# Layer norm ahead of attention: the statistics of the next image spread over units 7 to 22, the root replaced by a power of -0.5 on GpSimd

## The chip, the cores and the metric

The kernel runs on one core of a Trainium2 chip. The metric is the device time of one execution in microseconds (us). "Image" below is one of the eight 32x32 images with 384 channels (1,024 pixels each), numbered 0 to 7.

## The reference, cut to what matters

Three stages follow each other, each over all eight images. A convolution of group-normalised features comes first, and a feed-forward block comes last; neither is touched. The change is in the middle stage, attention with 12 heads of 32 channels:

```python
def _ln_t(v, eps=1e-05):
    m = jnp.mean(v, axis=-1, keepdims=True)
    s = jnp.var(v, axis=-1, keepdims=True)
    return (v - m) / jnp.sqrt(s + eps)

t = _to_tokens(x)                       # (8, 1024, 384)
t = t + _L1_attn_ref(_ln_t(t), Wq, Wk, Wv, Wo, bo)
```

The layer norm is over the 384 channels of each pixel. In the attention, q, k and v are projections of the normalised tokens, the softmax is over the 1,024 keys, and the result goes through Wo.

## The kernel before, in words

`attention_stage` keeps channels on the 128 partitions (three chunks, KC) and pixels on the free axis, in two halves of BANK = 512 pixels. After a prologue, which loads weights, normalises image 0 and projects it, each image goes through 24 **units** (`unit`, lines 966, 1143, 1277, 1375). A unit treats four heads, 256 queries and 512 keys in two halves e = 0, 1. Each engine runs its own hand-written list, and semaphores tie the lists together:

- TensorE, in each half: four score products (`scores`, L903) into two PSUM banks in turn, so that product n waits for exponential n-2; then `weigh` (L936, L944), which multiplies an earlier half's exponentials with v and with ones; then a `wave` (L919) of later scores into the four-bank tile `mx`.
- ScalarE: eight exponentials (L1232) of 128x512. VectorE: per half one `reduce_max` of `mx` (L1066); the next wave waits for it, as `mx` has one copy. GpSimd: four additions of exponentials (`add_pair`, L1356), which `weigh` waits for one unit later.

Other work lies between these. Units 6 to 23 project the next image (`project`, 18 items of nine 512-column products or of the same in 128-column pieces), through the single bank `pj`. Items come in threes of pairs q, k, v; the v items stand in units 10, 11, 16, 17, 22 and 23. ScalarE moves each item out (`stage_high`), VectorE takes the low part of q and k (`stage_low`, L1059). In units 6 to 21 an item is cut into four pieces that stand around the third score product of both halves; in 22 and 23 all of it stands in the first half. Units 0 to 5 put the previous image through Wo (`out_project`, L887), all in the second half; `move_out` takes it from `pj`, and GpSimd adds it (L1330). On odd units `move_pv` (L1240) copies `pv` and VectorE inverts the sums (`invert_sum`); on even units follow `attended` (VectorE), `attended_high` (ScalarE) and `attended_low` (GpSimd, L1320).

The layer norm of the image after the next takes these steps, for each half h of 512 pixels:

- `load_x` (SyncE, in unit 6) waits for the low parts of the image before. `fold_x` (GpSimd, units 18 and 20, L1334, L1337) adds the three chunks; `mean` (TensorE, L834, units 22 and 23) multiplies with 1/384 into `pj`; `centre` (VectorE, L1022) subtracts.
- In units 0 and 1 of the next image ScalarE squares a whole half in one instruction of 128x1536 (`square`, L1189) into the memory of `z[1]`, and GpSimd adds the chunks ahead of the unit's `add_pair` (`fold_squares`). `var` (L840, units 1 and 2) puts the mean square into `pj`, and `root` (L1194) takes the square root on ScalarE, before the fifth exponential of the unit.
- `invert_std` (VectorE, units 2 and 4) turns the root by 32x32 blocks, takes the reciprocal of one column per block (L1032) and turns it back over all columns; `normalise` (L1041) multiplies, units 3 to 5. `z_high` (ScalarE, L1201, units 4 and 5) rounds a whole half to float16, and `z_low` (VectorE, L1047, units 4 to 6) takes what is left. The projections of unit 6 on read both.

`schedule` (L689) writes units 6 to 23 of image b and 0 to 5 of image b+1 as the body of a loop, run six times; image 0's units 0 to 5 stand before it, and the rest of images 6 and 7 after it. The loop's jump lies between units 5 and 6. Image 7's units have no layer norm, and its units 6 to 23 no projection. The last image whose layer norm is made, image 7, is normalised in image 6. The prologue's end makes both means of image 1 (L961) before unit 0.

```python
for e in range(2):                                   # unit on TensorE, before
    scores(b, u, e, 0)
    if norm and u in (1, 2) and e == 0:
        var(b + 1, u - 1)
    if load and u >= IU - 2 and e == 1:
        mean(b + 2, u - IU + 2)
    scores(b, u, e, 1)
```

## Time and profile before

| | us |
|---|---|
| median of 3 runs (range) | 3006.07 (3001.13 to 3012.16) |
| the profiled execution, its own time | 3010.64 |
| its span, first to last instruction | 3008.7 |
| TensorE busy, matmuls | 2672.3 (89%) |
| VectorE busy | 1847.6 (61%) |
| ScalarE busy | 1586.1 (53%) |
| GpSimd busy | 1370.8 (46%) |
| mean granted TensorE clock | 0.949 |

The profiled execution took 1.9 us more than its span. Attention's first exponential starts at 475.64 us and its last at 2167.4 us. A unit is measured from its first exponential to that of the next unit; the boundaries 475.64, 685.80, 904.20, 1122.55, 1341.05, 1559.48, 1776.40 and 1986.60 are those of images 0 to 7. The clock column of a window is the share of full speed that was granted to TensorE, where 1.00 is 2.4 GHz and 0.5 is 1.2 GHz.

### The profile page before, as it was taken

To read this page: it belongs to the slowest core of one execution; us is meant where nothing else is said; L and a number is where in the kernel's file an instruction comes from. 1 tells how busy PE (TensorE), PEld (TensorE's weight loads), DVE (VectorE), ACT (ScalarE), POOL (GpSimd) and SP (SyncE) were. 2 spreads that over 40 slices of the span, in tenths; PEclk is the share of its full clock that TensorE was granted. 3 is DMA by queue.
4 is the path that set the end of the run, shared out by engine and by line. 5 is a ranking of instruction groups with operands and counts; after the bars stand their busy time and mean duration, and the time that the engine had idled before them with its cause. 6 is when DMAs were issued, how large, how long until landed. Compare 5 with 4: busy or idle time off the path is not lost. (4 is left out here: it accounts for less than half of the span.)

```text
span 3008.7 us, 64263 instructions
## 1 busy us (share of the span) xinstructions
PE 2672.3 (89%) x23600; PEld 1302.3 (43%) x23600; DVE 1847.6 (61%) x2360; ACT 1586.1 (53%) x2582; POOL 1370.8 (46%) x1096
## 2 busy tenths in 40 slices
PE   4989756998997997998988988998859999999999
PEld 3555322453453453543543544543324444444444
DVE  6766246887777787887777778777433333333332
ACT  2323024666666665666666666666534444444443
POOL 2222034676676676676676677677620101111110
PEclk9989877999998998998999999999979999999999
DMA  4233232111211211212112112111020101101010
GB/s 149 87 115 106 79 97 83 51 30 30 93 30 48 74 35 60 61 36 83 39 36 83 41 30 71 42 30 43 1 105 22 43 25 38 42 21 42 21 42 21
DMA packets 68634, 164.41 MB, mean 55 GB/s; under 512 B 13569, under 2 KB 17470, under 8 KB 67326
## 3 DMA queue, kind: packets, MB, share of 16 engines
q1 hardware_dynamic: 68350, 160.60, 16.8%
q8 instruction: 181, 2.97, 0.4%
q14 instruction: 103, 0.84, 0.1%
HBM read 59.13 MB, written 37.75 MB: 32 GB/s over the span
## 5 line engine op out<-in xcount | busy, mean ns | idle before, releaser
L1356 POOL TENSOR_TENSOR b_pair<-b_ex 128x512 f32<-128x512 f32 x768 | 975.3, 1295 | 517.9 <-ACT b_ex L1232 516.5
L1232 ACT ACTIVATE b_ex<-b_st 128x512 f32<-128x512 f32 x1536 | 866.4, 596 | 485.2 <-PE b_st L903 464.2
L1066 DVE TENSOR_REDUCE b_mxp<-b_mx 128x4 f32<-128x2048 f32 x384 | 876.9, 2284 | 322.4 <-PE b_mx L919 309.6
L903 PE MATMUL b_st<-b_qst,b_kst 97*128 97x256 f16 (+1 forms) x3072 | 548.0, 282 | 117.5 <-ACT b_ex L1232 83.1
L903 PEld LDWEIGHTS b_st<-b_qst,b_kst 97*128 97x128 f16 (+1 forms) x3072 | 235.1, 99 | 452.1 <-ACT b_ex L1232 255.5
L1601 DVE TENSOR_TENSOR c_gs<-c_g,c_gs 128x512 f16<-128x512 f32 x192 | 132.7, 691 | 482.0 <-ACT c_gs L1674 482.0
L936 PE MATMUL b_pv<-b_ex,b_v 128*32 128x256 f32 x6144 | 422.8, 394 | 0.0
L1522 PE MATMUL c_hid<-c_z,c_wi 128*128 128x512 f16 x1728 | 405.3, 380 | 11.3 <-DVE c_z L1594 11.3
L1537 PE MATMUL c_acc<-c_gs,c_wo 128*128 128x512 f16 x1728 | 404.0, 379 | 0.4 <-DVE c_gs L1601 0.4
L1670 ACT ACTIVATE c_g<-c_hid,c_bias 128x512 f32<-128x512 f32 x192 | 131.4, 684 | 363.5 <-PE c_hid L1522 363.3
L1522 PEld LDWEIGHTS c_hid<-c_z,c_wi 128*128 128x128 f16 x1728 | 169.3, 98 | 227.5 <-issue 18.8
L1537 PEld LDWEIGHTS c_acc<-c_gs,c_wo 128*128 128x128 f16 x1728 | 169.0, 98 | 204.5 <-ACT c_gs L1674 0.9
L944 PE MATMUL b_pv<-b_pair,b_ones 128*32 128x256 f32 x3072 | 241.6, 387 | 0.8 <-POOL b_pair L1356 0.8
L1707 POOL TENSOR_TENSOR c_xs<-c_x 128x512 f32<-128x512 f32 x16 | 21.3, 1334 | 478.6 <-DMA c_x<-after_attention 476.3
L936 PEld LDWEIGHTS b_pv<-b_ex,b_v 128*32 128x32 f32 x6144 | 163.1, 111 | 153.6 <-issue 81.5
L919 PE MATMUL b_mx<-b_kst,b_qst 32*128 32x512 f16 x1536 | 155.5, 395 | 35.9 <-DVE b_mxp L1066 32.4
L887 PE MATMUL b_pj<-b_ao,b_wo 128*128 128x512 f16 x432 | 115.0, 397 | 19.1 <-ACT b_xs L1194 14.7
L944 PEld LDWEIGHTS b_pv<-b_pair,b_ones 128*32 128x32 f32 x3072 | 101.4, 112 | 70.8 <-issue 6.1
L863 PE MATMUL b_pj<-b_z,b_wq 128*128 128x512 f16 x405 | 122.2, 397 | 10.5 <-DVE b_z L1047 7.7
L919 PEld LDWEIGHTS b_mx<-b_kst,b_qst 32*128 32x128 f16 x1536 | 38.8, 91 | 199.6 <-issue 147.1
L1674 ACT ACTIVATE c_gs<-c_g 128x512 f16<-128x512 f32 x192 | 120.9, 630 | 6.2
L308 PE MATMUL a_conv<-a_fs,a_wm 128*128 128x512 f16 x432 | 116.6, 421 | 0.0
(162 smaller groups left out, 2754.1 us busy)
## 6 DMA issues: line engine op xcount, KB each, us to landing
a_x<-in_x SPq DMA_DIRECT2D x8, 1536.0 KB, 6.9
a_ob<-a_x SPq DMA_DIRECT2D x8, 1536.0 KB, 7.2
after_conv<-a_ob SPq DMA_DIRECT2D x24, 512.0 KB, 2.6
b_xl<-after_conv SPq DMA_DIRECT2D x8, 1536.0 KB, 6.9
b_qst<-b_staged0q SPq DMA_DIRECT2D x192, 64.0 KB, 2.0
b_kst<-b_staged0k SPq DMA_DIRECT2D x192, 64.0 KB, 2.0
b_v<-b_vstaged SPq DMA_DIRECT2D x24, 512.0 KB, 3.0
b_xr<-after_conv SPq DMA_DIRECT2D x8, 1536.0 KB, 6.6
```

The lines of the kernel that those rows point to most:

```text
L863: last = nc.tensor.matmul(bank[:, :], ws[kind][a][:, k, g * P:(g + 1) * P], z[b][:, k, part * BANK:(part + 1) * BANK], start=n == 0, stop= ...
L903: last = nc.tensor.matmul(st[n % NST][:, j * QUERIES:(j + 1) * QUERIES], kst[g][0:depth, s, kt * P:(kt + 1) * P], qst[g][0:depth, s, q0:q0 ...
L919: last = nc.tensor.matmul(mx[:, s, :], qst[g][rows, s, q0 + t * P:q0 + (t + 1) * P], kst[g][rows, s, half * BANK:(half + 1) * BANK], start ...
L936: last = nc.tensor.matmul(pv[s * HEAD:(s + 1) * HEAD, 0:QUERIES], v[g][:, kt, s * HEAD:(s + 1) * HEAD], ex[u % 2][e][s][:, j * QUERIES:(j ...
L944: last = nc.tensor.matmul(pv[s * HEAD:(s + 1) * HEAD, QUERIES:BANK], ones[:, :], pair[u % 2][s][:, e * QUERIES:(e + 1) * QUERIES], start=F ...
L1066: nc.vector.reduce_max(mxp[x % 2][:, w // 2, :, w % 2], mx[:, :, :], AX_X).then_inc(mx_taken, 1)
L1232: nc.scalar.activation(ex[u % 2][e][s][:, :], st[n % NST][:, :], ACT.Exp, scale=SCALE).then_inc(exp_ready, 1)
L1356: nc.gpsimd.tensor_tensor(pair[u % 2][s][:, :], ex[u % 2][0][s][:, :], ex[u % 2][1][s][:, :], ALU.add).then_inc(pair_ready, 1)
L1522: last = nc.tensor.matmul(hid[m % NH][:, :], wi[a][:, k, m * P:(m + 1) * P], z[p][b][:, k, :], start=n == 0, stop=n == 8)
L1537: last = nc.tensor.matmul(acc[j][:, :], wo[a][:, m, j * P:(j + 1) * P], gs[m % NS][b][:, :], start=m == 0 and n == 0, stop=m == MC - 1 and ...
L1601: nc.vector.tensor_tensor(gs[m % NS][1][:, :], g[m % NG][:, :], gs[m % NS][0][:, :], ALU.subtract).then_inc(glo_ready, 1)
L1670: nc.scalar.activation(g[m % NG][:, :], hid[m % NH][:, :], ACT.Gelu, bias=bias[:, m:m + 1], scale=1.0 / WSCALE).then_inc(gelu_ready, 1)
```

## The change

Each step of the layer norm is done on one chunk of 512 columns and has a new place. For image b+2, in image b: `fold_x` in units 8 and 9, `mean` and `centre` in 10 and 11, `square` and `fold_square` in 12 to 15, `var` in 16 and 17, the inverse in 16 to 18, `normalise` in 18 to 21. In the next image's units 0 and 1 comes `z_high`, in units 0 to 2 `z_low`. The squares go into `xs` and into `std_turned` instead of `z[1]`. ScalarE's root is gone: VectorE turns the mean square out of PSUM, adds eps to one column per block, GpSimd raises the 128x16 column to -0.5, and VectorE turns it back. On TensorE the statistics stand in the second halves of the v units 10, 11, 16 and 17, whose item is put into the first half; units 22 and 23 are cut like the others; all items are cut 3, 2, 3, 1 instead of 2, 2, 2, 3 products, and the items through Wo are cut over both halves too, but for unit 3, where they stay in the second. In the prologue, image 1's statistics are made between the projections of image 0 through the score banks, and image 1 is normalised at its end; its load is issued ahead of the stacking copies. Waits and counts of semaphores follow.

```diff
+        def stat_bank(m, h):
+
+            return st[h] if isinstance(m, int) and m == 1 else bank_of(m, h)
+
+        def square_scratch(m):
+
+            return ot if in_prologue(m) else std_turned
+
+        V_UNITS = [FIRST + 6 * g + 4 + part for g in range(GROUPS) for part in range(2)]
+        MEAN_AT, VAR_AT = V_UNITS[0:2], V_UNITS[2:4]
...
                 for piece in range(PIECES + 1):
                     stack(0, 1, piece)
                 sp.wait_ge(w_low, 4)
                 load_r(0)
-                load_x(1)
                 sp.wait_ge(rows_set, 4 * GROUPS)
                 load_rows(0, 0)
...
+                    if i in (6, 7):
+                        mean(1, i - 6)
+                    if i in (13, 14):
+                        var(1, i - 13)
                     if i >= NQKV - AHEAD:
                         wave(0, i - NQKV)
...
+                first_half = qkv and u in MEAN_AT + VAR_AT
+                second_half = u == KC
 
                 for e in range(2):
                     scores(b, u, e, 0)
-                    if norm and u in (1, 2) and e == 0:
-                        var(b + 1, u - 1)
-                    if load and u >= IU - 2 and e == 1:
-                        mean(b + 2, u - IU + 2)
                     scores(b, u, e, 1)
-                    if item == 2:
-                        if e == 0:
+                    pieces = (0, 0), (0, 0)
+                    if first_half or second_half:
+                        if e == second_half:
+                            pieces = (0, 5), (5, 9)
+                    else:
+                        pieces = ((0, 3), (3, 5)) if e == 0 else ((5, 8), (8, 9))
+                    if begin and pieces[0][1]:
+                        if pieces[0][0] == 0:
                             if u == FIRST:
                                 pe.wait_ge(exp_ready, FILLS * (IU * b + u) + 1)
                             begin()
-                        part(2 * e, 4)
-                        scores(b, u, e, 2)
-                        part(2 * e + 1, 4)
-                    elif item == e:
-                        begin()
-                        part(0, 2)
-                        scores(b, u, e, 2)
-                        part(1, 2)
-                    else:
-                        scores(b, u, e, 2)
+                        part(*pieces[0])
+                    if load and u in MEAN_AT and e == 1:
+                        mean(b + 2, MEAN_AT.index(u))
+                    if load and u in VAR_AT and e == 1:
+                        var(b + 2, VAR_AT.index(u))
+                    scores(b, u, e, 2)
+                    if begin and pieces[0][1]:
+                        part(*pieces[1])
                     scores(b, u, e, 3)
                     if lagging(b, u, 2 - e):
...
                 if step == 0:
-                    dve.wait_ge(std_ready, 2 * m + h + 1)
-                    nc.vector.transpose(std_turned[:, :], std[h][:, :]).then_inc(inv_ready, 1)
-                if step == 1:
+                    dve.wait_ge(var_ready, 2 * m + h + 1)
+                    if not in_prologue(m):
+                        dve.wait_ge(sq_folded, 4 * m + 4)
+                    nc.vector.transpose(std_turned[:, :], stat_bank(m, h)[:, :]).then_inc(inv_ready, 1)
                     dve.wait_ge(inv_ready, at + 1)
-                    nc.vector.reciprocal(std_col[:, :], one_column(std_turned)).then_inc(inv_ready, 1)
+                    nc.vector.tensor_scalar(std_col[:, :], one_column(std_turned), EPS, None, ALU.add
+                                            ).then_inc(inv_ready, 1)
                 if step == 2:
-                    dve.wait_ge(inv_ready, at + 2)
+                    dve.wait_ge(inv_ready, at + 3)
                     nc.vector.transpose(std[h][:, :], over_columns(std_col)).then_inc(inv_ready, 1)
...
+                    if i in (7, 8):
+                        for k in range(KC):
+                            centre(1, i - 7, k)
+                    if i in (14, 15):
+                        for step in range(INVERSE):
+                            invert_std(1, i - 14, step)
...
                     for k in range(KC):
-                        centre(1, h, k)
+                        normalise(1, h, k)
...
+                    if u % 2 == 0 and n == 1 and lagging(b, u, 4):
+                        attended(b, (u - 4) // 2)
+                    if load and u in MEAN_AT and n >= 5:
+                        centre(b + 2, MEAN_AT.index(u), n - 5)
+                    if load and u == VAR_AT[0] and n >= 5:
+                        invert_std(b + 2, 0, n - 5)
+                    if load and (u, n) in ((VAR_AT[1], 5), (VAR_AT[1], 7), (VAR_AT[1] + 1, 2)):
+                        invert_std(b + 2, 1, (5, 7, 2).index(n))
+                    if load and (u, n) in ((18, 3), (18, 6), (19, 1)):
+                        normalise(b + 2, 0, (3, 6, 1).index(n))
+                    if load and (u, n) in ((19, 2), (20, 6), (21, 1)):
+                        normalise(b + 2, 1, (2, 6, 1).index(n))
                     if u % 2 and n >= 5 and lagging(b, u, 3):
                         invert_sum(b, (u - 3) // 2, n - 5)
-                    if u % 2 == 0 and n == 1 and lagging(b, u, 4):
-                        attended(b, (u - 4) // 2)
-                    if load and u >= IU - 2 and n == 7:
-                        for k in range(KC):
-                            centre(b + 2, u - IU + 2, k)
-                    if not norm:
-                        return
-                    if (u, n) in ((2, 2), (2, 5), (2, 6)):
-                        invert_std(b + 1, 0, (2, 5, 6).index(n))
-                    if (u, n) in ((3, 1), (3, 2), (3, 7)):
-                        normalise(b + 1, 0, (1, 2, 7).index(n))
-                    if (u, n) in ((4, 2), (4, 3), (4, 5)):
-                        invert_std(b + 1, 1, (2, 3, 5).index(n))
-                    if (u, n) in ((4, 6), (5, 2), (5, 3)):
-                        normalise(b + 1, 1, (6, 2, 3).index(n))
-                    if (u, n) in ((4, 7), (5, 1), (5, 7)):
-                        z_low(b + 1, 0, ((4, 7), (5, 1), (5, 7)).index((u, n)))
-                    if (u, n) in ((6, 2), (6, 3), (6, 6)):
-                        z_low(b + 1, 1, (2, 3, 6).index(n))
+                    if norm and (u, n) in ((0, 6), (0, 7), (1, 1)):
+                        z_low(b + 1, 0, (6, 7, 1).index(n))
+                    if norm and (u, n) in ((1, 7), (2, 2), (2, 3)):
+                        z_low(b + 1, 1, (7, 2, 3).index(n))
...
+            def square(m, h, k):
+                act.wait_ge(centred, KC * (2 * m + h) + k + 1)
+                wait(act, sq_folded, 4 * m + 2 * h + max(k - 1, 0))
+                if k == 1 and not in_prologue(m):
+                    act.wait_ge(inv_ready, 2 * NORMED * m)
+                into = xs[h] if k == 0 else square_scratch(m)
+                nc.scalar.activation(into[:, :], xl[:, k, h * BANK:(h + 1) * BANK], ACT.Square
                                      ).then_inc(squared, 1)
 
-            def root(m, h):
-                act.wait_ge(var_ready, 2 * m + h + 1)
-                nc.scalar.activation(std[h][:, :], bank_of(m, h)[:, :], ACT.Sqrt, bias=eps[:, 0:1]
-                                     ).then_inc(std_ready, 1)
...
+            def z_high(m, h, k):
+                act.wait_ge(z_ready, 6 * m + 3 * h + k + 1)
...
+                    if i in (8, 10):
+                        square(1, i // 2 - 4, 0)
+                        square(1, i // 2 - 4, 1)
+                    if i in (9, 11):
+                        square(1, i // 2 - 4, 2)
...
+                def beside(n):
+
+                    if load and 12 <= u < 16:
+                        h, step = u // 2 - 6, u % 2
+                        if n in (1, 5) and (step == 0 or n == 1):
+                            square(b + 2, h, 2 * step + n // 5)
+                    if norm and u < 2 and n in (1, 3, 5):
+                        z_high(b + 1, u, n // 2)
+                    if qkv and u >= FIRST and n == (2 if u in MEAN_AT + VAR_AT else 6):
+                        stage_high(b + 1, u - FIRST)
+                    if u % 2 and n == 3 and lagging(b, u, 3):
+                        move_pv(b, (u - 3) // 2)
+                    if u % 2 == 0 and n == 5 and lagging(b, u, 4):
+                        attended_high(b, (u - 4) // 2)
+                    if u < FIRST and out_proj and n == 7:
+                        move_out(b - 1, u)
+
+                for n in range(FILLS):
+                    exponential(b, u, n // HG, n % HG)
+                    beside(n)
...
+            def fold_square(m, h, k):
+                pool.wait_ge(squared, 3 * (2 * m + h) + k + 1)
+                wait(pool, sq_folded, 4 * m + 2 * h + k - 1)
+                nc.gpsimd.tensor_tensor(xs[h][:, :], xs[h][:, :], square_scratch(m)[:, :], ALU.add
+                                        ).then_inc(sq_folded, 1)
+
+            def invert(m, h):
+                pool.wait_ge(inv_ready, NORMED * (2 * m + h) + 2)
+                nc.gpsimd.tensor_tensor(std_col[:, :], std_col[:, :], power[:, :], ALU.pow).then_inc(inv_ready, 1)
+                pool.wait_ge(inv_ready, NORMED * (2 * m + h) + 3)
...
+                for h in range(HALVES):
+                    for k in (1, 2):
+                        fold_square(1, h, k)
+                for h in range(HALVES):
+                    invert(1, h)
...
-                if norm and u in (0, 1):
-                    fold_squares(b + 1, u)
                 for s in range(HG):
-                    if load and u in (18, 20) and s == 1:
-                        fold_x(b + 2, u // 2 - 9)
+                    if load and u in (8, 9) and s == 1:
+                        fold_x(b + 2, u - 8)
+                    if load and (u, s) in ((VAR_AT[0], 3), (VAR_AT[1], 3)):
+                        invert(b + 2, VAR_AT.index(u))
+                    if load and 12 <= u < 16 and s == 3 - u % 2 * 2:
+                        fold_square(b + 2, u // 2 - 6, 1 + u % 2)
```

## Rows read from the trace of the kernel before

**Rows 1.** Windows, image 3: length, busy us by engine, PEclk; units 0-8, 19, 22.

```profile
core 0: us, PE busy (x) PEld busy (x) DVE busy (x) ACT busy (x) POOL busy (x), PEclk, DMA share, GB/s
1122.55:1133.95 11.40, 8.38 (x82) 3.80 (x81) 10.33 (x11) 6.49 (x12) 8.98 (x9) 0.95 0.20 48
1133.95:1148.69 14.74, 11.40 (x84) 4.48 (x84) 5.37 (x6) 10.14 (x15) 9.55 (x9) 0.81 0.17 42
1148.69:1159.22 10.53, 8.80 (x85) 3.78 (x83) 7.43 (x13) 8.58 (x13) 4.78 (x5) 1.00 0.16 40
1159.22:1167.57 8.35, 7.78 (x83) 3.67 (x81) 8.28 (x8) 5.63 (x11) 7.07 (x8) 1.00 0.16 62
1167.57:1178.86 11.29, 9.35 (x83) 3.99 (x81) 9.88 (x15) 6.62 (x12) 6.63 (x5) 0.85 0.00 1
1178.86:1192.19 13.33, 8.19 (x83) 3.78 (x81) 10.71 (x11) 6.89 (x12) 11.16 (x9) 0.95 0.01 4
1192.19:1204.72 12.53, 11.16 (x83) 4.60 (x82) 8.62 (x14) 5.20 (x11) 3.28 (x3) 0.65 0.68 254
1204.72:1212.57 7.85, 7.78 (x83) 3.67 (x82) 5.88 (x6) 5.64 (x10) 6.03 (x6) 1.00 0.60 205
1212.57:1220.42 7.85, 7.78 (x83) 3.67 (x82) 6.88 (x12) 5.13 (x10) 4.96 (x5) 1.00 0.28 67
...
1298.63:1306.91 8.28, 7.77 (x83) 3.67 (x82) 5.88 (x6) 5.53 (x11) 8.17 (x8) 1.00 0.30 99
...
1323.04:1332.04 9.00, 8.53 (x112) 5.18 (x111) 8.14 (x14) 5.25 (x10) 5.17 (x5) 1.00 0.01 2
```

**Rows 2.** Windows: image 0 units 0-5, image 6 units 0-5 and 6-23, image 7 units 0-5, 6-18.

```profile
475.64:538.70 63.06, 44.38 (x366) 16.50 (x364) 45.62 (x54) 39.54 (x62) 35.20 (x28) 0.74 0.02 8
1776.40:1839.70 63.30, 52.13 (x492) 23.02 (x490) 50.35 (x57) 44.46 (x71) 45.09 (x37) 0.95 0.12 34
1839.70:1986.60 146.90, 140.45 (x1621) 73.56 (x1620) 115.26 (x144) 96.47 (x181) 97.22 (x83) 1.00 0.17 52
1986.60:2036.90 50.30, 46.41 (x486) 21.97 (x486) 34.45 (x43) 32.66 (x60) 38.49 (x34) 1.00 0.16 42
2037.09:2134.23 97.14, 80.29 (x937) 34.17 (x936) 75.34 (x94) 61.39 (x117) 68.55 (x59) 1.00 0.10 34
```

**Rows 3.** Timeline, unit 1 of image 3, PE and ScalarE: the root.

```profile
1139.53 1.28 ACT L1194 ACT_TABLE_LOAD   x1
...
1141.57 1.04 PE L887 MATMUL b_pj<-b_ao,b_wo 128*128 128x512 f16 x4 [2.10 <-ACT b_xs L1194]
```

**Rows 4.** Timeline, TensorE, units 5 to 6 of image 3.

```profile
1191.55 1.03 PE L903 MATMUL b_st<-b_qst,b_kst 97*128 97x256 f16 x4 [3.40 <-issue]
```

**Rows 5.** Instructions by line, VectorE on b_xl: ns min/median/max, first and last start.

```profile
L1041 DVE TENSOR_TENSOR b_xl<-b_xl,b_xs x48: 677/1178/1786, 399.5 to 1834.8; 128x512 f32<-128x512 f32 x48
L1047 DVE TENSOR_TENSOR b_z<-b_xl,b_z x48: 676/706/1777, 406.4 to 1848.3; 128x512 f16<-128x512 f32 x48
L1022 DVE TENSOR_TENSOR b_xl<-b_xl,b_pj x45: 648/677/689, 387.6 to 1776.3; 128x512 f32<-128x512 f32 x45
```

**Rows 6.** Timeline, TensorE's score matmuls, unit 22 of image 3.

```profile
1322.61 0.61 PE L903 MATMUL b_st<-b_qst,b_kst 97*128 97x256 f16 x4
...
1327.37 0.39 PE L903 MATMUL b_st<-b_qst,b_kst 97*128 97x256 f16 x2
```

**Rows 7.** Instructions by line, the reciprocal on VectorE and a GpSimd fold.

```profile
L1032 DVE RECIPROCAL b_std_col<-b_std_turned x16: 230/252/255, 398.5 to 1825.4; 128x16 f32<-128x16 f32 x16
...
L1337 POOL TENSOR_TENSOR b_xs<-b_xs,b_z x16: 1259/1278/2258, 392.5 to 1792.1; 128x512 f32<-128x512 f32 x16
```

**Rows 8.** Timeline, TensorE, end of the prologue and image 0's first scores.

```profile
462.48 0.40 PE L919 MATMUL b_mx<-b_kst,b_qst 32*128 32x512 f16 x4 [0.28 <-DVE b_mxp L1066]
...
474.97 1.06 PE L903 MATMUL b_st<-b_qst,b_kst 97*128 97x256 f16 x4
```

More of the change, by code:

```diff
@@ L769, in prologue @@
                 sp.dma_start(bo[:, :], b_o).then_inc(c_loaded, 16)
+                load_x(1)
                 for piece in range(PIECES + 1):
@@ L823, in _ @@
         def _(pe):
-            free = {id(pj): None, id(pv): None}
+            free = {id(bank): None for bank in (pj, pv, *st)}
             def take(bank, done, count):
@@ L860, in project_part @@
                 if kind < 2:
-                    for n in range(9 * piece // pieces, 9 * (piece + 1) // pieces):
+                    for n in range(n0, n1):
                         (a, b), k = PARTS[n // KC], n % KC
@@ L866, in project_part @@
                 else:
-                    for t in range(4 * piece // pieces, 4 * (piece + 1) // pieces):
+                    for t in range(4 * n0 // 9, 4 * n1 // 9):
                         at = (part * 4 + t) * P
@@ L881, in out_project, with out_part @@
                 pe.wait_ge(alo_ready, done)
-            def out_part(b, i, piece, pieces):
+            def out_part(b, i, n0, n1):
                 h, j = i // KC, i % KC
-                for n in range(9 * piece // pieces, 9 * (piece + 1) // pieces):
+                for n in range(n0, n1):
                     (a, c), k = PARTS[n // KC], n % KC
@@ L889, in out_part @@
                                             start=n == 0, stop=n == 8)
[L890 removed]
+                if n1 == 9:
                     last.then_inc(o_ready, 1)
@@ L972, in unit @@
                 if u < FIRST and out_proj:
                     begin = lambda: out_project(b - 1, u)
-                    part = lambda *piece: out_part(b - 1, u, *piece)
-                    item = 1
-                if u == FIRST and qkv:
-                    free[id(pj)] = (std_ready, 2 * b + 4)
+                    part = lambda n0, n1: out_part(b - 1, u, n0, n1)
+                if u == FIRST:
+                    free[id(pj)] = None
+                first_half = qkv and u in MEAN_AT + VAR_AT
@@ L1124, in prologue @@
                 weight_low(1)
+                for step in range(INVERSE):
+                    invert_std(0, 1, step)
                 for k in range(KC):
                     z_low(0, 0, k)
-                for step in range(INVERSE):
-                    invert_std(0, 1, step)
                 for k in range(KC):
@@ L1262, in weight_high @@
                                          ACT.Copy, scale=WSCALE).then_inc(w_high, 1)
-                square(0, 0)
+                for k in range(KC):
+                    square(0, 0, k)
                 weight_high(0)
-                root(0, 0)
-                square(0, 1)
+                for k in range(KC):
+                    square(0, 1, k)
                 weight_high(1)
-                root(0, 1)
-                z_high(0, 0)
+                for k in range(KC):
+                    z_high(0, 0, k)
                 weight_high(2)
-                z_high(0, 1)
+                for k in range(KC):
+                    z_high(0, 1, k)
                 weight_high(3)
```

123 lines of the change are left out of this document (41 added, 82 removed).

## The prediction

> **What bounds the kernel now.** I read the windows by unit first. In image 3 a unit away from the layer norm takes 7.85 us and TensorE is busy in 7.78 of them at full clock; VectorE has 5.88 on odd and 6.88 on even units, ScalarE 5.64 and 5.13 [rows 1]. There TensorE's list is the limit. In units 0 to 5 it is not: they take 11.40, 14.74, 10.53, 8.35, 11.29 and 13.33 us, 69.64 in all, and unit 6 takes 12.53 [rows 1]. The same six units in image 7, with the items through Wo and no layer norm, take 50.30 [rows 2].
>
> The timeline says how. In unit 1 ScalarE loads the root's table (1.28 us), takes the root and loads the exponential's again, and TensorE idles 2.10 us for `pj` [rows 3]. Squares of a whole half and their folds stand ahead of exponentials and pair sums, and in units 2 to 5 VectorE delays the waves that TensorE waits for. The clock falls after such pauses: 0.81 in unit 1, 0.85 in unit 4 [rows 1].
>
> Not all of unit 5 and 6 is layer norm. At the loop's jump TensorE stands 3.40 us with "issue" as its releaser [rows 4], and unit 6 then runs at 0.65 [rows 1]. The change doesn't touch the jump. Image 0's units 0 to 5 take 63.06, image 6's 63.30 [rows 2].
>
> **The change part by part**, for images 1 to 5 (image 3 stands for them; p is the time of the power on GpSimd).
>
> Units 0 to 5. With items in quarters over both halves, as in the steady units, six units take 6 x 7.85 = 47.1. Unit 3 keeps its item in one half: 50.30 / 6 = 8.38 [rows 2], so +0.5. The jump stays: +3.4. `z_high` comes in pieces behind exponentials 1, 3 and 5, where ScalarE waits for scores anyway; only unit 0's second half is full (three moves beside four exponentials): +0.4. `z_low` is six instructions of 0.71 median, 1.78 at most [rows 5], in units 0 to 2; VectorE has there about 6.2, 5.2, 6.2 (the steady values less `stage_low`) and 4.2 to 7 more, 22 to 25 in 23.6, and unit 2 holds two of them behind its fullest half: +1.0. Sum 52.4 against 69.64: **17.2 gained**. All squares, folds, roots and table loads are gone from here; late next is only the wave of unit 2.
>
> Unit 6. `z_low` leaves it, but it is slow by the clock, and the jump's pause before it stays. I take 0; it could be 4.7 (12.53 to 7.85).
>
> Units 7 to 23 take 218.50 - 69.64 - 12.53 = 136.3 now. After:
> - 17 x 7.85 = 133.4. This includes units 22 and 23, 9.00 each now [rows 1].
> - The two folds of x move from 18 and 20 to 8 and 9: +0.4, as in unit 19 (8.28) [rows 1], where GpSimd's late `attended_low` holds `move_pv`. SyncE issues the load of x in unit 6; unlike before it is not held by unit 6's `z_low`, so one unit and a half cover it. If that cover were gone, GpSimd would stand in unit 8 with the pair sums behind it.
> - Four v units with the item in the first half: that half takes 4.76 (1322.61 to 1327.37) [rows 6], instead of 3.93 (half of 7.85). The statistic, two products of about 0.5 us, stands after the second score product, while ScalarE does its exponentials, in a half without an item: free. 4 x 0.85 = +3.4.
> - The projection of unit 12 waits for the last `centre`: VectorE has three of 0.68 [rows 5] and the sum's inverse behind unit 11's second wave. +0.4.
> - Squares in 12 to 15, one chunk each: +0.6, since in even units' second halves ScalarE gets four exponentials and three other items. The square of chunk 2 also waits for GpSimd's fold of chunk 1; queued behind it are exponentials 2 and 3, which have about a microsecond to spare.
> - The inverse of unit 16: VectorE's turning back stands at the unit's last place and waits for the power, which GpSimd comes to only after three pair sums (each about 1.28, as [rows 7]). Behind that wait stands the maximum of the next wave, and TensorE waits for it: 0.5 + p. In unit 18 the same step comes a unit later and hides p up to about 3 us.
> - Units 18 to 21: VectorE has 2 x (5.88 + 6.88) = 25.5, one more turn (about 0.7) and six `normalise` of 1.18 [rows 5]: 33.3 in 31.4. +2.0, the slack of a wave being used up by then.
>
> No row has a power on GpSimd. An add of 512 columns takes 1.28 there [rows 7], so 16 columns scaled by size give 0.04, the lower end; nothing bounds it above but that a power is a function, not an add. I take p = 1.0, near the full-size add, and keep 0.04 to 4 in the range. The Trainium skill ("GPSIMD Engine Reference", section 4.1) says the opposite of what this edit does: elementwise arithmetic belongs on VectorE, as GpSimd is about twice as slow. Taken at its word with VectorE's reciprocal of 16 columns (0.25) [rows 7], p would be 0.5 and the whole 5 us better. It doesn't list a power.
>
> Sum for units 7 to 23: 133.4 + 0.4 + 3.4 + 0.4 + 0.6 + 1.5 + 2.0 = 141.7, so **5.4 lost**. Net 11.8 per image, five times: 59.
>
> Image 0: its units 0 to 5 have no item through Wo; units without any item take 97.14 / 13 = 7.47 [rows 2]. 6 x 7.47 = 44.8, +1.4 for z, +0.8 for entering the loop, +2 for six `normalise` at the prologue's end ahead of the first maximum: 49 against 63.06, 14 gained. Less 5.4: 8.6.
>
> Image 6: units 0 to 5 as above but without a backward jump, 49.8 against 63.30: 13.5. Units 6 to 23 have no statistics: 146.90 against 18 x 8.0 = 144 (its own steady unit): 2.9. Sum 16.4. Image 7: 50.30 against 47.6: 2.7.
>
> Prologue: between its last wave (462.48) and the first scores (474.97) [rows 8] TensorE mostly waits for image 1's load, folds and means. About 11 us go. Against that stand four statistics between the projections (4), centring and inverses on VectorE among the waves (3 to 5, and p), and the earlier start of the projections without the root (-2). I take 4 gained.
>
> In all 59 + 8.6 + 16.4 + 2.7 + 4 = 91. The profiled execution took 3010.64, the median 3006.07; 3010.64 - 91 is 2920, and less the 4.6 between them 2915. I forecast 2917.
>
> **The rivals.**
> - *VectorE is too full.* `normalise` meets GpSimd's pair sums and took up to 1.79 [rows 5]. Six at 1.79 add 3.7, and if TensorE then pauses long enough in units 16 to 21 for its clock to fall, as in units 1 and 4, that costs about 1.6 each time (unit 4: 9.35 busy instead of 7.78 [rows 1]). 3.7 + 2 x 1.6 = 7 in six images: 42, so 2959. For it: 33.3 of 31.4. Against: before, units 2 to 5 held as much. Chance 0.2.
> - *The clock comes back in unit 6*, since units 0 to 5 reach the jump without pauses of their own: 4.7 x 5 = 23; with VectorE's overrun partly absorbed (2 x 6 = 12) 2882. Against it stands the pause of 3.40 alone. The Trainium skill ("TensorE: Matmul & The Clock Gate", Part 1) has the slow clock as the default that activity lifts, and by that rule the jump's pause would be enough to lose it. Chance 0.17.
> - *The power is slow* (slower than before). each of the 16 columns takes GpSimd long; place: units 16 to 18 of six images, and four times in the prologue. Cost 10(p - 1) + 6(p - 3), which eats 91 at p = 7.4 us: from there the change loses. At p = 10 it is 132, so 3049. For it: no row prices it, and pair sums queue behind. Against: one column per block is all it gets. Chance 0.05.
> - *It moves nothing*: the stalls only change places, and the image stays near 218. For it: unit 5 and 6's excess is the loop's. Against: image 7's 50.30. About 3000, chance 0.03.
>
> **How the numbers follow.** Forecast 0.55, at 2917, with its own range 2895 to 2945 (p from 0.04 to 4: -10 to +36, VectorE's overrun 0 to 12, the prologue 5 either way). With the first two rivals 2875 to 2965 holds 8 in 10. A measurement can tell about 0.5% (15 us) from no change: faster 0.92, same 0.03, slower 0.05.
>
> **What would show it.** Right: units 0 to 2 near 8 to 9 us; no table load in the loop; units 22 and 23 at 7.85; units 10, 11, 16, 17 near 8.7; unit 18 or 19 longer by about 1; unit 6 still slow at a clock near 0.65; an image of some 207 us. Wrong: the image above 214; GpSimd's power over 4 us; new windows below 0.9 of the clock in units 16 to 21; GpSimd waiting for `load_x` in unit 8; TensorE waiting for `z_high` in unit 0.

## The result and the profile after

The changed kernel takes 2930.12 us, the median of 4 runs (2926.13 to 2937.41), against 3003.60 (2995.23 to 3012.16) for the kernel before beside it: a ratio of 0.9758, 95% interval 0.9723 to 0.9793. A repeat gave 0.9770. The forecast was 2917, its range 2875 to 2965. The median is 73.5 us lower, and 67.5 in the repeat. The profiled execution took 2929.51 us with a span of 2927.6; VectorE is busy for 1849.9 us, ScalarE for 1533.7, GpSimd for 1418.2.

The windows of image 3 by unit, as in [rows 1]: units 0, 1, 2, 3, 5, 6, 7, then 10, 11, 16, 17, 18, 19.

```profile
core 0: us, PE busy (x) PEld busy (x) DVE busy (x) ACT busy (x) POOL busy (x), PEclk, DMA share, GB/s
1087.76:1095.24 7.48, 7.48 (x83) 3.59 (x82) 7.14 (x10) 6.55 (x13) 4.72 (x5) 1.00 0.29 67
1095.24:1103.77 8.53, 7.54 (x83) 3.59 (x82) 8.46 (x8) 6.84 (x13) 7.73 (x7) 1.00 0.35 82
1103.77:1115.59 11.82, 7.61 (x83) 3.50 (x81) 10.98 (x14) 5.30 (x11) 10.40 (x9) 1.00 0.15 36
1115.59:1125.43 9.84, 9.27 (x83) 4.08 (x82) 5.58 (x6) 5.73 (x10) 5.09 (x5) 0.83 0.14 55
...
1132.91:1143.10 10.19, 7.54 (x83) 3.50 (x81) 5.87 (x6) 5.63 (x11) 9.53 (x9) 1.00 0.02 5
1143.10:1155.00 11.90, 10.57 (x83) 4.33 (x82) 6.49 (x11) 5.13 (x11) 3.46 (x4) 0.71 0.66 250
1155.00:1162.48 7.48, 7.48 (x83) 3.60 (x82) 5.65 (x6) 5.54 (x11) 5.59 (x6) 1.00 0.61 242
1178.25:1186.82 8.57, 8.48 (x112) 5.09 (x110) 8.34 (x12) 5.15 (x11) 7.71 (x7) 1.00 0.23 53
1186.82:1196.25 9.43, 8.58 (x112) 5.10 (x110) 7.14 (x9) 5.54 (x11) 5.43 (x6) 1.00 0.31 97
...
1227.25:1235.66 8.41, 8.41 (x112) 5.19 (x111) 7.67 (x12) 5.16 (x10) 6.19 (x6) 1.00 0.24 57
1235.66:1248.35 12.69, 10.05 (x112) 5.81 (x111) 7.60 (x9) 5.54 (x11) 9.96 (x8) 0.87 0.24 58
1248.35:1257.86 9.51, 7.55 (x83) 3.60 (x82) 9.01 (x13) 5.17 (x11) 8.48 (x7) 1.00 0.09 23
1257.86:1265.34 7.48, 7.48 (x83) 3.60 (x82) 7.41 (x9) 5.54 (x11) 4.53 (x4) 1.00 0.30 99
```

The units near 7.48 at full clock are those in which nothing disturbs TensorE. Units 0 to 5 take 55.3 us (1087.76 to 1143.10; 69.64 before), unit 6 11.90 (12.53), units 7 to 23 140.9 (136.3): the image takes 208.1 instead of 218.5. Five units are far above their neighbours: 2, 3, 17 and, on both sides of the loop's jump, 5 and 6. In 17 the clock is 0.87 and in 3 0.83, each after a pause of TensorE (2.64 us in unit 17, 3.67 at the end of unit 2).

The units 0 to 5 of images 0, 6 and 7, as in [rows 2]:

```profile
474.29:522.36 48.07, 36.57 (x360) 14.44 (x360) 39.15 (x46) 30.10 (x58) 29.72 (x24) 0.86 0.04 14
1712.58:1765.20 52.62, 46.97 (x488) 21.88 (x486) 43.78 (x49) 35.23 (x66) 40.00 (x33) 0.97 0.16 42
1907.97:1954.56 46.59, 45.94 (x487) 21.43 (x485) 35.31 (x43) 32.53 (x60) 37.58 (x33) 1.00 0.18 47
```

From the profiled execution of before to that of after, 81.1 us are gone. By the first exponentials of the images, 1.4 of them come from what lies ahead of image 0, 12.7 from image 0 (197.4 instead of 210.2), 49.7 from images 1 to 5, 14.8 from image 6, and 2.4 from image 7. The profiled execution of before lies at the high end of its runs (3010.64 in 2995.23 to 3012.16), so that 81.1 is more than the medians show. And the attention does not start at the same time in each execution: its first product for a mean comes at 385.49 before and at 386.44 after, but at 382.20 in the repeat. From there to the first exponential it is 90.2 us before, 87.9 after and 88.6 in the repeat.

The timeline of units 16 and 17 has the costliest new wait:

```profile
1236.47 2.92 POOL L1364 TENSOR_TENSOR b_std_col<-b_std_col,b_power 128x16 f32<-128x16 f32 x1
...
1239.42 0.71 DVE L1050 STREAM_TRANSPOSE b_xs<-b_std_col 128x512 f32<-128x512 f32 x1 [4.10 <-POOL b_std_col L1364]
...
1240.06 2.25 DVE L1079 TENSOR_REDUCE b_mxp<-b_mx 128x4 f32<-128x2048 f32 x1
...
1242.37 0.40 PE L929 MATMUL b_mx<-b_kst,b_qst 32*128 32x512 f16 x4 [2.64 <-DVE b_mxp L1079]
...
1242.81 2.29 DVE L1079 TENSOR_REDUCE b_mxp<-b_mx 128x4 f32<-128x2048 f32 x1 [0.50 <-PE b_mx L929]
```

GpSimd comes to the power at 1236.47 and takes 2.92 us for it. VectorE stands 4.10 us at the turn back; behind it in its list stands a wave's maximum (L1079), and TensorE waits 2.64 us for that (L929). Three rows by instruction follow, each with ns min/median/max: the power, `z_low`, and, for comparison, a turn of 32x32 blocks with one input (L1102).

```profile
L1364 POOL TENSOR_TENSOR b_std_col<-b_std_col,b_power x16: 2899/2914/2921, 399.4 to 1664.5; 128x16 f32<-128x16 f32 x16
```

```profile
L1062 DVE TENSOR_TENSOR b_z<-b_xl,b_z x48: 650/1723/1773, 410.8 to 1735.6; 128x512 f16<-128x512 f32 x48
```

```profile
L1102 DVE STREAM_TRANSPOSE b_inv<-b_pvs x96: 428/434/445, 505.6 to 2093.2; 128x256 f32<-128x256 f32 x96
```

### The profile page after: what moved, and what is told of

Its sections match the earlier page's. It is cut to its first block and busy times, and to the rows that moved or that the text cites. A ratio compares the mean times of both kernels' runs of the same rounds, so it can differ in the third digit from the quotient of the medians.

```text
span 2927.6 us, 64485 instructions
## 1 busy us (share of the span) xinstructions
PE 2624.0 (90%) x23600; PEld 1287.3 (44%) x23600; DVE 1849.9 (63%) x2359; ACT 1533.7 (52%) x2602; POOL 1418.2 (48%) x1113
## 5 line engine op out<-in xcount | busy, mean ns | idle before, releaser
L1372 POOL TENSOR_TENSOR b_pair<-b_ex 128x512 f32<-128x512 f32 x768 | 979.8, 1301 | 440.4 <-ACT b_ex L1244 439.2
L1079 DVE TENSOR_REDUCE b_mxp<-b_mx 128x4 f32<-128x2048 f32 x384 | 876.6, 2283 | 222.2 <-PE b_mx L929 208.2
L913 PE MATMUL b_st<-b_qst,b_kst 97*128 97x256 f16 (+1 forms) x3072 | 541.3, 280 | 58.8 <-ACT b_ex L1244 35.8
L913 PEld LDWEIGHTS b_st<-b_qst,b_kst 97*128 97x128 f16 (+1 forms) x3072 | 226.3, 98 | 367.2 <-ACT b_ex L1244 203.9
L929 PE MATMUL b_mx<-b_kst,b_qst 32*128 32x512 f16 x1536 | 153.4, 389 | 77.6 <-DVE b_mxp L1079 75.8
L929 PEld LDWEIGHTS b_mx<-b_kst,b_qst 32*128 32x128 f16 x1536 | 38.7, 91 | 241.5 <-issue 125.3
```

Source lines behind the costliest of these rows:

```text
L913: last = nc.tensor.matmul(st[n % NST][:, j * QUERIES:(j + 1) * QUERIES], kst[g][0:depth, s, kt * P:(kt + 1) * P], qst[g][0:depth, s, q0:q0 ...
L929: last = nc.tensor.matmul(mx[:, s, :], qst[g][rows, s, q0 + t * P:q0 + (t + 1) * P], kst[g][rows, s, half * BANK:(half + 1) * BANK], start ...
L1079: nc.vector.reduce_max(mxp[x % 2][:, w // 2, :, w % 2], mx[:, :, :], AX_X).then_inc(mx_taken, 1)
L1372: nc.gpsimd.tensor_tensor(pair[u % 2][s][:, :], ex[u % 2][0][s][:, :], ex[u % 2][1][s][:, :], ALU.add).then_inc(pair_ready, 1)
```

## The experiments

**Repeat.** The changed kernel once more.

> The changed kernel again, beside which the others of this call are read. 2926 to 2937 us. In image 3 units 2, 3, 17 and 18 again take about 11.8, 9.8, 12.7 and 9.5 us, if these are the fixed effect of the order and not of one execution.

Measured: 2931.87 us, ratio 0.9770 (0.9746 to 0.9794), and the same length in every steady unit. Units 2, 3, 17 and 18 of image 3 take 12.2, 9.7, 12.7 and 9.5 us, as expected but for 0.4 us in unit 2.

**The turn back one place later.**

```diff
-                    if load and u == VAR_AT[0] and n >= 5:
-                        invert_std(b + 2, 0, n - 5)
+                    if load and (u, n) in ((VAR_AT[0], 5), (VAR_AT[0], 7), (VAR_AT[0] + 1, 2)):
+                        invert_std(b + 2, 0, (5, 7, 2).index(n))
```

> VectorE turns the first half's power back in unit 17 behind the third exponential's place instead of at the end of unit 16. Theory 1 (VectorE stands 4.1 us for GpSimd's power at unit 16's last place, and the wave's maximum queued behind it holds TensorE 2.64 us and costs its clock): the wait goes, unit 17 falls from 12.7 to 8.5 to 9 us, unit 18 by up to 0.5, six times: 24 to 30 us less than the changed kernel. Rival (the power itself holds GpSimd, and late pair sums hold TensorE, so the place of the turn is not what counts): unit 17 stays above 12, no change within 5 us.

Measured: 2928.17 us, 0.9762 (0.9737 to 0.9787), no gain. Unit 17 falls from 12.7 to 8.8 us, as the first theory has it, but 18 rises to 12.5 and 19 from 7.5 to 9.8. The timeline of unit 18, VectorE, GpSimd and TensorE's next wave:

```profile
1244.29 2.78 DVE L1094 TENSOR_SCALAR b_shift<-b_top_turned 8x32 f16<-8x32 f32 x4 [0.31 <-DVE b_top_turned L1088]
...
1244.51 3.74 POOL L1372 TENSOR_TENSOR b_pair<-b_ex 128x512 f32<-128x512 f32 x3 [0.16 <-POOL b_std_col L1364]
...
1247.09 1.44 DVE L1114 TENSOR_TENSOR b_pvs<-b_pvs,b_inv 128x256 f32<-128x256 f32 x1
...
1249.65 2.27 DVE L1079 TENSOR_REDUCE b_mxp<-b_mx 128x4 f32<-128x2048 f32 x1
...
1251.98 0.61 PE L929 MATMUL b_mx<-b_kst,b_qst 32*128 32x512 f16 x4 [4.55 <-DVE b_mxp L1079]
```

The turn still waits 1.77 us for the power in its new place, but no wave waits behind it. GpSimd's three pair sums (L1372) are late because of the powers and now lie beside VectorE's chain for the sums. Four moves of 8x32 (L1094) that take 0.17 us each alone take 2.78 together, the product L1114 1.44 instead of 0.42. The maximum at 1249.65 comes late and TensorE stands 4.55 us. So the rival is right in the late pair sums and in the missing gain, but not in unit 17. GpSimd's three sums keep their 1.25 each: it isn't that both slow down, VectorE waits.

**The old cut of the items.** All items that are cut over both halves in 2, 2, 2, 3 products again, the rest of the change kept.

```diff
-                        pieces = ((0, 3), (3, 5)) if e == 0 else ((5, 8), (8, 9))
+                        pieces = ((0, 2), (2, 4)) if e == 0 else ((4, 6), (6, 9))
...
-                    for t in range(4 * n0 // 9, 4 * n1 // 9):
+                    for t in range((4 * n0 + 4) // 9, (4 * n1 + 4) // 9):
```

> All items are cut 2, 2, 2, 3 products again. A q or k unit took 7.48 us after and 7.85 before. Theory 1 (three products between the second and third score product fill the wait for the exponential, two leave TensorE idle, and the last piece of one instead of three ends the unit sooner): the steady unit goes back to 7.85, some 16 units per image and 0.35 each, 35 to 40 us slower than the changed kernel. Rival (the shorter unit comes from elsewhere, such as the moved statistics): units stay at 7.48, no change within 5 us.

Measured: 2964.94 us, 0.9877 (0.9853 to 0.9902): 33 us slower than the repeat beside it (35 to 40 expected). Unit 7 of image 3, then the start of that unit in the changed kernel and here:

```profile
1167.69:1175.54 7.85, 7.78 (x83) 3.68 (x82) 5.88 (x6) 5.63 (x11) 5.59 (x6) 1.00 0.53 215
```

```profile
1155.00 2.34 ACT L1244 ACTIVATE b_ex<-b_st 128x512 f32<-128x512 f32 x4 [0.80 <-PE b_st L913]
1155.02 0.81 PE L873 MATMUL b_pj<-b_z,b_wq 128*128 128x512 f16 x3
1155.64 0.12 PEld L913 LDWEIGHTS b_st<-b_qst,b_kst 97*128 97x128 f16 x2 [0.31 <-ACT b_ex L1244]
```

```profile
1167.70 0.60 PE L873 MATMUL b_pj<-b_z,b_wq 128*128 128x512 f16 x2
1168.33 0.11 PEld L913 LDWEIGHTS b_st<-b_qst,b_kst 97*128 97x128 f16 x2 [0.53 <-ACT b_ex L1244]
```

The third score product writes into the bank that the unit's first exponential reads, so its weights (L913) are loaded only when that exponential, 0.60 us long, has ended. In both kernels that is 0.62 to 0.63 us after the item's first product. Three products, one each 0.22 us, fill this time and two leave some 0.2 us of it empty, in each half of the unit: that is the 0.37 us, as the first theory has it. The busy column doesn't show the pause, since it counts a product longer (0.38 us) than the distance to the next.

**`z_low` one at a time.** The same six instructions in six different half units.

```diff
-                    if norm and (u, n) in ((0, 6), (0, 7), (1, 1)):
-                        z_low(b + 1, 0, (6, 7, 1).index(n))
-                    if norm and (u, n) in ((1, 7), (2, 2), (2, 3)):
-                        z_low(b + 1, 1, (7, 2, 3).index(n))
+                    if norm and (u, n) in ((0, 6), (1, 2), (2, 6)):
+                        z_low(b + 1, 0, u)
+                    if norm and (u, n) in ((3, 2), (4, 6), (5, 2)):
+                        z_low(b + 1, 1, u - 3)
```

> The six z_low go one to a unit's half, in units 0, 1, 2, 3, 4 and 5 instead of two each in units 0, 1 and 2. Theory 1 (in unit 2 two of 1.7 us stand ahead of the second wave's maximum, TensorE idles 3.67 us and its clock falls): units 2 and 3 go from 11.8 and 9.8 to 8 and 8.4, 25 to 32 us less than the changed kernel over six images. Rival (z_low costs the same wherever it meets GpSimd's pair sums, since VectorE is full in all these units): the loss spreads, less than 10 us gained.

Measured: 2890.23 us, 0.9628 (0.9604 to 0.9652), 41.6 us faster than the repeat, more than the 25 to 32 expected. First unit 2 as it was in the changed kernel, then the windows of units 1 and 2 here:

```profile
1108.96 4.73 POOL L1372 TENSOR_TENSOR b_pair<-b_ex 128x512 f32<-128x512 f32 x3 [1.42 <-ACT b_ex L1244]
...
1109.12 3.45 DVE L1062 TENSOR_TENSOR b_z<-b_xl,b_z 128x512 f16<-128x512 f32 x2
...
1112.50 2.28 DVE L1079 TENSOR_REDUCE b_mxp<-b_mx 128x4 f32<-128x2048 f32 x1
...
1114.83 0.40 PE L929 MATMUL b_mx<-b_kst,b_qst 32*128 32x512 f16 x4 [3.67 <-DVE b_mxp L1079]
```

```profile
1082.43:1089.91 7.48, 7.48 (x83) 3.60 (x82) 7.25 (x8) 6.84 (x13) 7.48 (x7) 1.00 0.39 93
1089.91:1097.56 7.65, 7.55 (x83) 3.51 (x81) 7.42 (x11) 5.22 (x10) 6.60 (x6) 1.00 0.03 7
```

In the changed kernel two `z_low` take 3.45 us beside three pair sums, the maximum behind them starts at 1112.50 and the wave waits 3.67. Apart, units 1, 2 and 3 take 7.48, 7.65 and 8.34 us instead of 8.53, 11.82 and 9.84. The collisions haven't gone (the median of L1062 is still 1424 ns); there is only never more than one of the six ahead of a maximum.

**A cheap instruction in place of the power.** GpSimd multiplies the 16 columns instead; this leaves out the power, and so the values of the layer norm.

```diff
-                nc.gpsimd.tensor_tensor(std_col[:, :], std_col[:, :], power[:, :], ALU.pow).then_inc(inv_ready, 1)
+                nc.gpsimd.tensor_tensor(std_col[:, :], std_col[:, :], power[:, :], ALU.mult).then_inc(inv_ready, 1)
```

> GpSimd multiplies the 128x16 column by -0.5 instead of raising it to -0.5; the output is not the reference's. Theory 2, after the run that turned later (a power of 2.91 us makes GpSimd's pair sums late, and VectorE's small moves and products in units 17 and 18 then stand behind them, as there where four moves of 0.17 took 2.78): with a product of 0.1 to 0.3 us both the wait and the lateness go, units 16 to 18 take 8.4, 8.5 to 9 and 8 to 8.5 instead of 8.4, 12.7 and 9.5, some 5 us per image and 30 in all less than the changed kernel, about 2900. Rival (VectorE is full by its own work there: 33.3 us in 31.4): unit 18 still over 9.5, 10 us less at most.

Measured: 2891.59 us, 0.9651 (0.9630 to 0.9673). Units 17 and 18 of image 3:

```profile
1212.05:1220.46 8.41, 8.41 (x112) 5.18 (x111) 6.82 (x6) 5.54 (x10) 5.81 (x7) 1.00 0.37 88
1220.46:1230.05 9.59, 7.55 (x83) 3.61 (x82) 9.02 (x15) 5.25 (x11) 7.30 (x8) 1.00 0.09 22
```

The multiplication takes 0.22 us (212 to 222 ns). Unit 17 takes 8.41 us instead of 12.69 and keeps its clock; 4.28 us in six images are 26. Unit 18 stays at 9.59, above the 8 to 8.5 expected: that part is VectorE's own work, as the rival has it. The first exponential comes at 461.6 instead of 474.3. Of these 12.7 us, 4.3 lie ahead of the attention's first product for a mean (382.15 against 386.44), where both kernels do the same; 8.4 are the prologue's. So the power as it is placed costs some 34 us over a multiplication by the traces, and 40 by the medians (2931.87 less 2891.59); a quarter of the 34 lies ahead of image 0.

**The root back on ScalarE, the rest of the spread kept.** Root at the ends of units 16 and 17, reciprocal on VectorE.

```diff
+            def root(m, h):
+                act.wait_ge(var_ready, 2 * m + h + 1)
+                nc.scalar.activation(std[h][:, :], stat_bank(m, h)[:, :], ACT.Sqrt, bias=eps[:, 0:1]
+                                     ).then_inc(std_ready, 1)
...
+                    if load and u in VAR_AT and n == 7:
+                        root(b + 2, VAR_AT.index(u))
...
-                    if load and (u, s) in ((VAR_AT[0], 3), (VAR_AT[1], 3)):
-                        invert(b + 2, VAR_AT.index(u))
```

> The spread over units 7 to 22 is kept, but ScalarE takes the root again, now at the end of units 16 and 17, with its two table loads each; VectorE takes the reciprocal and there is no power on GpSimd. Theory (the spread carries the gain, and the power is no better than a root that stands where its 3.25 us are needed least): units 17 and 18 take 10 to 11 each, where they took 12.7 and 9.5: within 10 us of the changed kernel either way. Rival (the missing root is what the change gains by, since table loads stop the exponentials): 5 us or more per root, over 2960.

Measured: 2911.25 us, 0.9712 (0.9696 to 0.9728). Units 16 to 18 take 10.5, 10.1 and 7.5 us, 28.0 against 30.6 with the power, and the first exponential comes at 462.0. So the spread, with the new cut, brings the gain; the exchange of engines, as it was placed, cost about 20 us (2931.87 less 2911.25; by the ratios 17). Expected was a difference within 10.

**The kernel before with the new cut alone**, for q and k in units 6 to 21.

```diff
+    CUTS = (0, 3, 5, 8, 9)
...
-                    for n in range(9 * piece // pieces, 9 * (piece + 1) // pieces):
+                    for n in (range(*CUTS[piece:piece + 2]) if pieces == 4 else range(9)):
```

> The kernel before with one part of the change: q and k items in units 6 to 21 are cut 3, 2, 3, 1 products instead of 2, 2, 2, 3. Theory 1: the steady q or k unit falls from 7.85 to 7.48, 10 or 11 units per image in seven images, 24 to 28 us less than before. Rival (only together with the rest): no change within 5 us.

Measured: 2977.44 us, 0.9935 (0.9918 to 0.9952). Unit 9 of image 3:

```profile
1201.04:1208.52 7.48, 7.48 (x83) 3.59 (x82) 5.66 (x6) 5.54 (x10) 5.60 (x6) 1.00 0.20 47
```

The steady unit is 7.48 us here too. The cut is worth 20 us in the kernel before (2997.34 beside it) and 33 in the changed one, where it reaches more items.

**The power ahead of the first pair sum**, with `z_low` apart as above. GpSimd takes the power at the head of units 17 and 18, the turns back follow at (17, 5) and (18, 6), and `normalise` is spread one by one to unit 23.

```diff
-                    if load and (u, s) in ((VAR_AT[0], 3), (VAR_AT[1], 3)):
-                        invert(b + 2, VAR_AT.index(u))
+                    if load and (u, s) in ((VAR_AT[0] + 1, 0), (VAR_AT[1] + 1, 0)):
+                        invert(b + 2, VAR_AT.index(u - 1))
```

> Built on the kernel with z_low apart. GpSimd's powers go ahead of the first pair sum of units 17 and 18, where it waits for exponentials some 2.2 us; VectorE turns back in 17 and 18's second halves, and the six normalise go one to a half, in units 18 to 23. Theory 2: neither VectorE nor the pair sums wait, units 16 to 18 take 8.4, 8.5 and 8 to 9 instead of 8.4, 12.7 and 9.5: 20 to 30 us less than the kernel with z_low apart (2890), so 2860 to 2870. Rival (a power of 2.91 is longer than GpSimd's idle time, so pair sums are late in any place): one unit of 17 to 19 stays above 11, less than 8 us gained.

Measured: **2861.90 us**, 0.9546 (0.9530 to 0.9562); image 3 takes 196.9. Windows of units 17 and 18, then rows of their timeline:

```profile
1199.71:1208.12 8.41, 8.41 (x112) 5.18 (x111) 5.91 (x6) 5.54 (x11) 8.15 (x7) 1.00 0.37 88
1208.12:1217.09 8.97, 7.61 (x83) 3.61 (x82) 8.43 (x14) 5.24 (x11) 8.70 (x6) 1.00 0.02 5
```

```profile
1202.37 2.90 POOL L1364 TENSOR_TENSOR b_std_col<-b_std_col,b_power 128x16 f32<-128x16 f32 x1
...
1205.53 4.97 POOL L1372 TENSOR_TENSOR b_pair<-b_ex 128x512 f32<-128x512 f32 x4 [0.26 <-POOL b_std_col L1364]
...
1206.36 0.70 DVE L1050 STREAM_TRANSPOSE b_xs<-b_std_col 128x512 f32<-128x512 f32 x1
...
1212.83 0.78 DVE L1094 TENSOR_SCALAR b_shift<-b_top_turned 8x32 f16<-8x32 f32 x4 [0.31 <-DVE b_top_turned L1088]
```

The power takes the same 2.90 us, but it lies where GpSimd waited 2.2 to 2.5 us for the unit's first exponentials before. The first of the four pair sums behind it waits 0.26 us, and the turn (L1050) finds it done. Units 16 to 19 take 8.4, 8.4, 9.0 and 8.4. The four moves of L1094, free of pair sums here, take 0.78 together. Three things changed at once over `z_low` apart, the places of the power, of the turns and of `normalise`, and the power's place was not run by itself. What bears on it: in image 3 units 16 to 19 take 38.1 us in the changed kernel, 33.9 there with the cheap instruction, and 34.2 here.

**Root against power with everything apart.** The last kernel with ScalarE's root of the one before.

> The spread order of e8_power_first with ScalarE's root in place of the power (root at the ends of units 16 and 17, reciprocal on VectorE). Theory 1 (a well placed power costs GpSimd's time only, a root costs two table loads and the exponentials behind them): units 16 to 18 take 10.5, 10.1 and 7.5 us as in e5_root_back, 28.1 in all against 8.4 + 8.4 + 9.0 = 25.8 in e8_power_first, +14 us over six images; the first exponential comes at 462.0 instead of 474, -12; so the two cancel: 2855 to 2875, the same as e8_power_first within 0.5%. Theory 2 (the power is never worth it: its four column steps crowd VectorE and GpSimd in any place): 2840 to 2850, with units 19 to 21 at 7.5 where e8_power_first has 8.4 in unit 19. Theory 3 (the table loads collide with the spread normalise): over 2880.

Measured: 2864.53 us, 0.9549 (0.9533 to 0.9565), the same as with the power; the first of the three theories holds. Units 16 and 17 of image 3, where the table loads are:

```profile
1188.94:1199.39 10.45, 9.77 (x130) 6.10 (x128) 8.72 (x12) 8.40 (x14) 8.24 (x8) 1.00 0.27 65
1199.39:1209.48 10.09, 8.40 (x95) 4.31 (x95) 6.75 (x8) 8.79 (x14) 5.59 (x5) 1.00 0.22 54
```

Units 16 to 19 take 35.5 us against 34.2 with the power, and the first exponential comes at 462.5 against 471.9.

**The prologue's turns apart**, in the fastest kernel so far.

```diff
-                    if i in (14, 15):
-                        for step in range(INVERSE):
-                            invert_std(1, i - 14, step)
+                    if i in (14, 16):
+                        invert_std(1, i // 2 - 7, 0)
                     if NQKV - AHEAD <= i < NQKV - 1:
                         take_wave(0, i - NQKV)
+                    if i in (15, 17):
+                        invert_std(1, i // 2 - 7, 2)
```

> e8_power_first with image 1's inverse in the prologue taken apart: the turn of the mean square stands after items 14 and 16, the turn back one item later, behind a wave's maximum, so that no maximum waits behind GpSimd's power. Theory 1 (the 3.02 and 3.08 us that VectorE waits for the power hold the maxima, and through them TensorE for 5.84 and 3.18 us): the first exponential comes 6 to 9 us before 474, the rest of the kernel is unchanged, 2853 to 2856 against 2861.9. Theory 2 (the end of the prologue is set by something else, the normalise of image 1 or the moves of the items): first exponential within 1 us of 474, 2861 to 2863.

Measured: 2858.70 us, 0.9527 (0.9511 to 0.9543). First the turn back and the wave that waits behind it in the changed kernel, then that wave here:

```profile
458.16 0.71 DVE L1050 STREAM_TRANSPOSE b_xs<-b_std_col 128x512 f32<-128x512 f32 x1 [3.02 <-POOL b_std_col L1364]
```

```profile
461.11 0.61 PE L929 MATMUL b_mx<-b_kst,b_qst 32*128 32x512 f16 x4 [5.84 <-DVE b_mxp L1079]
```

```profile
457.35 0.52 PE L929 MATMUL b_mx<-b_kst,b_qst 32*128 32x512 f16 x4 [2.13 <-DVE b_mxp L1079]
```

The kernel with the power first has the same wait of 5.84 us. It falls to 2.13, and the first exponential comes at 465.8 instead of 471.9, as the first theory has it. But unit 0 of image 0 rises from 7.6 to 10.1 us, against that theory, since a wave now waits 3.90 us for its maximum there, so the time falls by 3.2 only, and the two intervals overlap: the trace shows the step, the times don't settle its worth. It is the fastest kernel here, by a margin too small to claim.

## Why the prediction was right, and where its steps were not

The sign and the place of the gain held, for the reason given: the layer norm leaves units 0 to 5, where VectorE and ScalarE delayed the waves, and an image takes 208.1 us for 206.6. The size was somewhat less, 73.5 us by the medians where 89 was forecast (3006.07 to 2917). That it came so near is in part luck, as large errors of opposite sign lie in it: the new cut, without a term of its own, gained 20 to 33 us, and `z_low` beside the pair sums and the power behind them cost about 42 and 34 to 40, where the sum had about 6 and 10 for them. In units 7 to 23 of image 3 the steady unit gives 6.3 us more than forecast, what is added to it costs 13.7 instead of 8.3, and 140.9 for 141.7 is left.

- **Units 0 to 5**: 55.3 us for 52.4. Units 0 and 4 take 7.48. The failed term is the +1.0 for unit 2. It stood on six `z_low` of 4.2 to 7 us in all; they take 1.72 each (median), about 10 us, since they now lie beside the pair sums. Units 1 to 3 lost 7 us by it, which moving it alone gave back, 41.6 us in the whole. The rival of a too full VectorE named this mechanism and its fall of the clock, but for `normalise` in units 18 to 21.
- **Unit 6**: 11.90 for 12.53, the clock 0.71. The rival of a returning clock fell; only in image 4 are they 9.99 and 0.83. The pause at the jump is 2.65 us for 3.40.
- **The steady unit** is the largest error in units 7 to 23: 17 x 7.85. The cut of 3, 2, 3, 1 stood in the change and I gave it no term. It makes the unit 7.48, worth 17 x 0.37 = 6.3 us, and shown by both runs on the cut.
- **The power**: p = 1.0 was mis-sized, it is 2.91 (2899 to 2921 ns), inside the bounds of 0.04 to 4 and far from the 0.5 that was weighed beside them. Nor did 16 columns scale by size: their multiplication takes 0.22, not 0.04. The term for unit 16's wait would be 0.5 + p = 3.4 with the right p; measured are 4.3 in unit 17 (12.69 against 8.41 with the cheap instruction), the half clock in a part of it included. That the power also makes the pair sums behind it late, so that moving the turn one place gained nothing, was not in the sum. With p = 2.91 the prediction's own terms give about 19 us more, 2936; for p = 4 they give 2953, beyond the upper end of 2945 that it took.
- **Units 18 to 21**: +2.0, measured +2.0, all of it in unit 18 (9.51 against 7.48), and there with the cheap instruction too. Units 19 to 21 are steady.
- **Units 10, 11, 16**: 8.57, 9.43 and 8.41 against a steady 7.48, so +1.1, +2.0 and +0.9 for +0.85 each. In unit 11 TensorE also waits 0.85 us for `centre` ahead of the item. Unit 12 has 8.04, +0.6 for +0.4. The folds of x cost 0.8 in unit 9 (8.29) for 0.4, squares in 13 to 15 0.5 for 0.6, and units 22 and 23 take 7.78, +0.3 each where the sum had nothing.
- **Image 0** gained 12.7 for 8.6: units 0 to 5 take 48.1 for 49, and units 6 to 23 lose 2.2 for 5.4. **Image 6** gained 14.8 for 16.4: units 0 to 5 take 52.6 for 49.8, with unit 2 as slow as in the others. **Image 7** gained 2.4 for 2.7: units 0 to 5 take 46.6 for 47.6, but unit 7 rises from 7.5 to 8.9.
- **Prologue**: 1.4 gained for 4, or 2.3 from the attention's first mean on. The 3 to 5 us and p for VectorE among the waves was too small: VectorE waits twice about 3.0 us for the power ahead of maxima, and TensorE 5.84 and 3.28 us behind it.
- **Slow power**: the point from which the change loses was p = 7.4; at 2.91 no run came near it.
- **Signs**: of those for right, unit 2 (11.8) and unit 17 (12.7) failed. One of those for wrong came true, a window below 0.9 of the clock in units 16 to 21: unit 17 with 0.87, by the wait for the power.

## What to carry to other kernels

A slow instruction is charged for its neighbours: ask what stands behind it in its own queue and behind its reader in theirs, and put it where its engine idles. Here the power behind three pair sums cost 34 to 40 us over a multiplication. With the power at the head of a unit, and the work around it spread, units 16 to 19 took 34.2 us against 33.9 with the multiplication, and the whole kernel as long as with a root on ScalarE. An instruction moved beside another engine's work must be priced at its longest duration there, not at its median from the old place. And an order of pieces that looks like bookkeeping (3, 2, 3, 1 for 2, 2, 2, 3) gets a term of its own.

## What the runs showed of the hardware

A power of 128x16 on GpSimd takes 2.91 us, over twice an add of 128x512 there (median 1.27), with 1/32 of the columns, and 13 times a multiplication of the same 16 columns (0.22).

While a GpSimd addition of two SBUF tiles runs, some VectorE instructions wait for its end and then run at their usual pace. Two SBUF inputs: `z_low` 0.65 us alone, 1.72 beside pair sums; L1114 0.42 and 1.44. Even moves of 8x32 with one input: 0.17 and up to 1.21. In the run with the later turn the last of three pair sums ends at 1248.25, and L1114, begun at 1247.09, at 1248.53. Turns of one input (428/434/445) and the maximum, which reads PSUM (2.25 to 2.29), keep their time; 93 of the 96 turns of L1102 start while GpSimd runs an instruction. Pair sums are held too: 47 of 768 take 1.4 to 1.8 us instead of 1.25, and 37 of these start while a `z_low` or a `normalise` runs. The Trainium skill ("SBUF — State Buffer", section "Who interferes with whom") has it so: VectorE and GpSimd share one pair of ports, held by one of them for a whole instruction, which VectorE needs for a second input or in its fast two-port modes, and reductions don't. The traces agree, those of the 8x32 moves included if they are in such a mode, which no row shows. What the lock costs in all was not tried by itself: no run took GpSimd's pair sums away.

The pause at the loop's jump stays: after unit 5 TensorE stands 2.65 us with "issue" as its releaser (2.6 to 2.9 in images 1 to 5), and unit 6 follows at 0.71 of the clock. Images 0 and 6 have no backward jump there; their unit 6 has no such pause and takes 8.3 us at full clock. No run here took the jump away. It is the largest rest, unit 5 and 6 being together 5 to 7 us above two steady units in images 1 to 5.
